# Layer 1 attention: both halves of a batch of transposed probabilities are split in one slot

## The reference

```python
q = rmsnorm((x @ Wq + bq), gq); k = rmsnorm((x @ Wk + bk), gk); v = x @ Wv + bv
scores = q @ k.T / sqrt(128)
attn = softmax(scores)
out = attn @ v            # all heads side by side: 1024 x 4096
return out @ Wo + bo
```

## Time and profile before

| | |
|---|---|
| median of 3 runs | 3316.5 us |
| profiled execution | 3324.06 us, its span 3322.2 us |
| mean granted TensorE clock | 0.985 of full speed |
| PE, PEld busy | 2993.8 us (90%), 2684.5 us (81%) |
| DVE busy | 2018.2 us (61%) |
| POOL busy | 1582.9 us (48%) |
| ACT busy | 1346.1 us (41%) |
| layer 1 attention, steady part | from about 1310 to about 3000 us of the span |

### The profile page before, as it was taken

The page is one execution under the profiler, slowest core; times in us unless marked ns, Lnnn a source line. Parts: engine busy times, 40 slices in busy tenths (PEclk is TensorE's granted clock), DMA queues, the critical chain, the costliest instruction groups (busy, mean ns, idle before and its releaser), DMA issues. The chain is left out here.

```text
span 3322.2 us, 57041 instructions
## 1 busy us (share of the span) xinstructions
PE 2993.8 (90%) x17632; PEld 2684.5 (81%) x17632; DVE 2018.2 (61%) x3189; ACT 1346.1 (41%) x2375; POOL 1582.9 (48%) x1075
## 2 busy tenths in 40 slices
PE   7999999999999887888888888888888888886998
PEld 7989999899899767778787788888887888875786
DVE  3445544544455557666677666677776677774555
ACT  3333333333333223445444544454444454443221
POOL 3333333333333413555555555555555555553765
PEclk9999999999999989999999999999999999998999
DMA  4121121211111111334343434343343343334551
GB/s 126 52 60 56 57 59 49 60 58 51 60 55 53 29 36 54 99 96 105 94 105 95 105 95 105 95 106 98 99 104 87 95 105 97 101 88 131 153 142 54
DMA packets 225483, 279.66 MB, mean 84 GB/s; under 512 B 48256, under 2 KB 124048, under 8 KB 225296
## 3 DMA queue, kind: packets, MB, share of 16 engines
q1 hardware_dynamic: 224576, 278.11, 31.5%
q10 hardware_dynamic: 816, 0.79, 0.1%
q0 software_dynamic: 32, 0.02, 0.0%
HBM read 125.63 MB, written 2.10 MB: 38 GB/s over the span
## 5 line engine op out<-in xcount | busy, mean ns | idle before, releaser
L1343 ACT ACTIVATE b_prob<-b_s_ps,b_shift 128x1024 f32<-128x1024 f32 x256 | 285.9, 1117 | 562.9 <-DVE b_shift L1491 562.9
L1281 POOL TENSOR_TENSOR pT_lo<-pT_lo,pT_hi 128x1024 fp32r<-128x1024 f32 x128 | 305.2, 2385 | 166.7 <-ACT pT_hi L1338 166.7
L1281 POOL TENSOR_TENSOR b_pT_lo<-b_pT_lo,b_pT_hi 128x1024 fp32r<-128x1024 f32 x128 | 304.9, 2383 | 160.7 <-ACT b_pT_hi L1338 160.7
L82 PE MATMUL b_pj_kq<-b_w_hi,xT_hi 128*128 128x384 f32 x1008 | 346.1, 343 | 8.5 <-DVE b_nat L1461 8.5
L83 PE MATMUL b_pj_kq<-b_w_lo,xT_hi 128*128 128x384 f32 x1008 | 344.1, 341 | 0.0
L84 PE MATMUL b_pj_kq<-b_w_hi,xT_lo 128*128 128x384 f32 x1008 | 344.1, 341 | 0.0
L1499 DVE STREAM_TRANSPOSE b_blocks<-b_prob 128x1024 f32<-128x1024 f32 x256 | 316.3, 1235 | 2.6 <-ACT b_prob L1343 2.6
L506 ACT ACTIVATE a_sig<-a_pj 128x512 f32<-128x512 f32 x192 | 115.1, 600 | 485.8 <-PE a_pj L84 485.8
L82 PE MATMUL a_pj<-b_w_hi,xT_hi 128*128 128x256 f32 x1024 | 295.3, 288 | 12.6 <-DVE xT_lo L647 11.6
L1491 DVE TENSOR_REDUCE b_shift<-b_s_ps 128x1 f32<-128x1024 f32 x256 | 303.7, 1187 | 2.7 <-PE b_s_ps L84 2.7
L84 PE MATMUL a_pj<-b_w_hi,xT_lo 128*128 128x256 f32 x1024 | 289.6, 283 | 0.0
(11 more groups left out here) (257 smaller groups left out, 8948.4 us busy)
## 6 DMA issues: line engine op xcount, KB each, us to landing
pT_lo<-b_blocks SPq DMA_DIRECT2D x1024, 64.0 KB, 2.0
b_pT_lo<-b_blocks SPq DMA_DIRECT2D x1024, 64.0 KB, 2.0
b_w_raw<-in_w SPq DMA_DIRECT2D x32, 768.0 KB, 4.4
b_w_raw<-in_w SPq DMA_DIRECT2D x95, 256.0 KB, 3.2
a_k_raw<-a_k_blocks SPq DMA_DIRECT2D x512, 32.0 KB, 1.8
a_w_raw<-in_w SPq DMA_DIRECT2D x32, 256.0 KB, 2.6
a_ow_raw<-in_ow SPq DMA_DIRECT2D x32, 256.0 KB, 3.1
b_ow_raw<-in_ow SPq DMA_DIRECT2D x32, 256.0 KB, 2.7
```

The source lines that it names most:

```text
L82: pe.matmul(out, w_hi, x_hi, start=first, stop=False)
L1281: pool.tensor_tensor(pT_lo[i % 2][:, :, cut, :], f(pT_lo[i % 2][:, :, cut, :]), f(pT_hi[i % 2][:, :, cut, :]), ALU.subtract).then_inc(pT_l ...
L1343: act.activation(prob[t % 2][:, :], s_ps[t % 2][:, :], ACT.Exp, bias=shift[:, t:t + 1], accum_out=row_sum[:, t:t + 1]).then_inc(exp_done, 1)
```

## The change

`split_part` becomes `split_batch`. It returns a batch in the even slots only, and ACT and POOL then split both parts of it one behind the other. The products on PE stay where they were.

```diff
-        def split_part(h, cur, rest, s):
-
-            n = (s - 4) % 8
+        def split_batch(h, cur, rest, s):
+
+            if s % 2:
+                return None
             if s >= 4:
-                return (h, n // 2, n % 2) if cur else None
-            return (h - 1, n // 2, n % 2) if rest else None
+                return (h, (s - 4) // 2) if cur else None
+            return (h - 1, (s + 4) // 2) if rest else None
...
-                    if split_part(h, cur, rest, s):
-                        prob_lo(*split_part(h, cur, rest, s))
+                    if split_batch(h, cur, rest, s):
+                        for part in range(2):
+                            prob_lo(*split_batch(h, cur, rest, s), part)
...
-                    if split_part(h, cur, rest, s):
-                        prob_hi(*split_part(h, cur, rest, s))
+                    if split_batch(h, cur, rest, s):
+                        for part in range(2):
+                            prob_hi(*split_batch(h, cur, rest, s), part)
```

## The result

| | before | after |
|---|---|---|
| median | 3322.66 us (4 runs, 3315.22 to 3330.63) | 3226.59 us (4 runs, 3224.19 to 3232.02) |
| profiled execution, its span | 3324.06, 3322.2 us | 3225.75, 3224.0 us |
| ratio | | 0.9713, 95% interval 0.9681 to 0.9744 |

The forecast was 3231 us (3195 to 3290). The kernel became 96 us faster in the medians and 98 us in the spans. DVE's first and last sum of squares of layer 1 lay 1712.9 us apart before (1254.9 to 2967.8) and 1614.4 us after (1253.8 to 2868.2), so all of it lies in this attention.

A forecast was written before the change was run, and what follows sets the result against it. No engine was full, so waits decided: PE's late part 1 and the path PE, DVE, ACT. PE's earliness was worth 86 us, the moves on POOL and ACT nothing: 3316.5 - 86, rounded to 3231 us, range 3195 to 3290.

The forecast's parts named there:

- PE's wait for part 1 goes from the path: PE between a batch's two product parts: part 1 could start 3.6 us sooner, worth 86 us over the layer.
- Why POOL was late with part 1: POOL in odd slots: the weights' (1.30 us) and values' (0.75 us) low parts stand ahead of part 1's subtraction.
- The root takes over: DVE's scaling in even slots: 0.70 us of the take's wait for PE turns into a wait for POOL's root.
- PE keeps waiting 135 us for POOL: PE before part 1: needing 11.9 us of a 12.9 us batch, it still waits some 135 us, down from 221.6.
- ACT's copy is hidden, with 0.04 us to spare in slot 0: ACT before even slots' exponential: the second copy's 1.0 us fits in idle time, leaving 0.97 us in slot 4, 0.04 in slot 0.
- POOL's move is free: POOL's other low parts, moved behind part 1, end before the next mean and are read in later slots: cost zero.
- the transfers' loop doesn't bind: Loop through transposition, transfers, ACT's copy, POOL's subtractions and PE: 12.0 us a batch, under the 12.9 expected.
- 2 us of cover on POOL: POOL in slot 3: low parts with output weights end at 2032.2, 2 us before the next mean at 2034.3.
- Fewer collisions: DVE's scaling against POOL's subtraction: the 0.4 us gap in slot 4 widens, so fewer collisions than now (some six).
- the rival: Scaling collides with POOL's doubled subtraction, held for both, 4.1 us at most; 131 us lost against 86 won, 3361 us; chance 0.07.

The follow-up runs named there:

- e10b: Kernel before the change, plus a wait: POOL's subtraction of part 0 waits until DVE's scaling is done; 3311.01 us, 0.995 of the kernel before.
- e11b: Changed kernel, plus a wait: POOL's subtraction of part 0 waits until DVE's scaling is done; 3227.15 us.
- e1: ACT's half of the change alone: ACT copies both parts in the even slot, POOL subtracts part 1 in the odd slot as before; 3400.88 us, 1.0254 to before.
- e2: POOL's half of the change alone: POOL subtracts both parts in the even slot, ACT copies part 1 in the odd slot as before; 3361.85 us, 1.0119 to before.
- e8: Changed kernel with an extra, unused copy of part 1 on ACT between its two copies; 3252.84 us, 0.9798 to before.
- e4: Changed kernel with DVE's transposition in odd slots moved ahead of the keys' and queries' low parts; 3133.25 us, 0.9431 to before.
- e7b: Changed kernel with DVE's scaling moved behind the even slot's maximum, into POOL's two subtractions; 3203.8 us in a single execution.

## Why the prediction was right

The gain was 96 us in the medians where 86 was forecast. That 3231 lies only 4 us from the measured 3226.59 is in part luck: it was taken off a median of 3316.5 us, and with one execution more the kernel before stands at 3322.66. From there 86 us less is 3237.

- **PE's wait for part 1 goes from the path**: right. What it is worth was the main term, 86 us for a measured 96. In quiet heads it is 2.6 and 3.0 us a head by turns, 2.8 on average, against the 2.7 that 86 us over 32 heads gave; `e10b` against `e11b` gives 3311.0 - 3227.2 = 84 us for the loop alone. The rest is a term that the sum left out, though the rows showed it: held scalings and low clock of the kernel before. Of the 98 us between the spans, the four heads of 53.9 to 61.1 us hold 15 more than 2.8 each.
- **Why POOL was late with part 1**: half right. The low parts ahead of it set its start in two batches of four. In the two others POOL was done with them and stood 0.84 us (median of 63 waits) for ACT's copy of part 1, which the prediction did not name. Its change moved both, and `e1` and `e2` show that neither half gives the gain.
- **The root takes over**: right in kind, 64.1 us measured in 124 waits, 0.52 each where the working had 0.70. From the mean's end to the scaling it is 1.20 us in the rows above, 1.17 in the working. But the take starts 0.10 us after the mean, and the trace counts idle time from its end, after 0.56 us, where the working let it hold DVE for 0.48 from the mean on.
- **PE keeps waiting 135 us for POOL**: wrong. PE waits 40.4 us there. Part of the room shows in other waits. The matmuls wait 33.6 us for the projection's PSUM tile, which the take frees (8.5 before), and 20.9 us for DVE's `x_nat` (6.3 before). With the 40.4 that makes 95 us of the 135. Weight loads, which overlap matmuls (2662.2 us busy beside their 3027.8 in a span of 3224.0), stand 47.6 us for the same tile (none before) and 64.0 us before the product with the output weights (8.8 before), where the profile names nothing that they wait for. A wait on an engine that doesn't bound moves to whatever ends last, and its place was not worked out.
- **ACT's copy is hidden, with 0.04 us to spare in slot 0**: right. The exponential's wait is 465.0 us, forecast 475. `e8` showed that the spares are real, and that the overrun counts half.
- **POOL's move is free; the transfers' loop doesn't bind**: right, and by its trace `e4` reached that loop at 12.1 us a batch where the working had 12.0. The 2 us of cover on POOL were misjudged for slot 3. The output weights' low part doesn't follow the others at once, but starts at 2027.23 in the head above and ends 0.11 us before the root. It did so before the change too (0.10 us), so this costs nothing.
- **Fewer collisions**: right in sign, none of 4 left. The price named for the rival, both subtractions, was wrong by `e7b`. The prediction read that the scaling ended as the subtraction did; in its own rows it ended 0.54 us later (2535.22 and 2534.68), as in `e1` and `e7b`. The cause of a collision, a take that comes late, was named better than its weight: with half the change it made the kernel slower by 2.5%, which nothing in the prediction foresaw. It is what the change would have met had only one engine's order been changed.

## What to carry to other kernels

A wait of the busiest engine is worth only what the engines waiting behind it can use: subtract, at each of them, the next releaser (here 0.7 us of POOL's root out of 1.4). A split of work over two engines has to be moved on both, since half the move can be worse than none (2.5% and 1.2% slower here). And an edit that does nothing may be worth much once another is made: the reordering on DVE gave 0 us before the change and 93 after it.

## What the runs showed of the hardware

- DVE's scaling (128x512, `b_nat` and `b_rstd`) lasted 2.21 to 2.92 us, median 2.38, instead of 0.69 in the 38 cases of `e1` from 1310 us on in which it issued while POOL's 128x1024 subtraction ran. It ended 0.54 to 0.56 us after that subtraction in all 38. In `e7b`, where a second subtraction followed at once, it ended as long after the first in 116 cases (1.32 us long in the slot shown), and the second lasted 2.83 to 2.87 us instead of 2.40. In the three cases of `e1` in which the subtraction started up to 0.4 us after the scaling, the scaling kept its 0.68 us and the subtraction took 2.57 to 2.81 us (2.81 at 1481.59).
- Other DVE instructions kept their time beside the same subtraction: in `e1` the take lasted 0.54 to 0.56 us there in 89 cases, the transposition 1.22 to 1.25 in 79, the maximum 1.18 to 1.23 in 174, as without it. What sets the scaling apart from them is shown by no run.
- In `e1`, 48 stands before part 1 between 1310 and 2970 us lasted 2.3 to 3.1 us. Behind 33 of them all or some matmuls of the product were 0.21 us apart instead of 0.12 (granted clock 0.50 in the stretch of 1999.2 to 2001.8 us), behind none of the 68 shorter ones. In the kernel before the shortest stand followed by the slow spacing was 1.89 us, and 26 of 27 stands of 2.0 us and one of 3.6 were not followed by it; in `e2` the shortest was 1.76 us (clock 0.51 from 1806 to 1808.5 us). After the change the stands before part 1 were at most 1.04 us in the steady part, and the clock was 1.00 from 1500 to 2800 us.
